# Layer zero's experts with the hidden values produced transposed: up weights loaded per tile, scaling moved to ACT

## What is computed

```python
xn = _rms_norm(x, scale)                                # x: the layer-normed input
ids = argmin(_dist2(xn, centroids), axis=-1)            # one of 8 experts per token
for e in range(8):
    h = einsum('bsd,dh->bsh', xn, up_w[e])              # 128 -> 512
    a, g = split(h, 2, axis=-1)                         # 256 and 256
    y = einsum('bsh,hd->bsd', a * silu(g), down_w[e])   # 256 -> 128
    out = where(ids == e, y, out)
out = out + skip
```

## Time and profile before

| | us |
|---|---|
| median of 3 runs | 1212.86 (1212.7 to 1213.04) |
| the profiled execution's own time | 1209.96 |
| its span, first to last instruction | 1207.7 |

### The profile page before, as it was taken

How to read it: one execution, slowest core, us unless ns; L and a number is a source line. 1 busy time by engine, 2 the same in 40 slices (tenths; PEclk the granted TensorE clock), 3 DMA queues, 4 the chain that set the end, 5 groups by cost and what they waited for, 6 DMA issues and landing times.

```text
span 1207.7 us, 28517 instructions
## 1 busy us (share of the span) xinstructions
PE 1069.6 (89%) x8602; PEld 685.4 (57%) x8602; DVE 958.7 (79%) x2148; ACT 879.5 (73%) x2187; POOL 790.2 (65%) x1147
## 2 busy tenths in 40 slices
PE   2666369989996689999999999999999999999986
PEld 1555247767774455656565556555555665565553
DVE  6779989979995578888887888788778788888861
ACT  2555338767875378888888888888788888888874
POOL 4476668668775366667666776677667766776641
PEclk9766689999997699999999999999999999999998
DMA  9511112112111322333233323332232223322310
GB/s 274 154 39 37 34 52 57 45 46 54 49 51 32 99 66 66 90 81 84 65 89 78 88 66 81 81 92 66 66 94 81 78 69 92 87 72 69 88 37 11
DMA packets 148172, 89.35 MB, mean 74 GB/s; under 512 B 73080, under 2 KB 137272, under 8 KB 147768
## 3 DMA queue, kind: packets, MB, share of 16 engines
q1 hardware_dynamic: 143928, 79.01, 25.0%
q0 software_dynamic: 4096, 8.53, 2.4%
HBM read 55.91 MB, written 31.47 MB: 72 GB/s over the span
## 4 chain that ended last, share of the span: by engine, by line
PE 52%; issue 5%; ACT 4%; DVE 4%; DMA 2%; POOL 0%; SPq 0%; another core or an unknown queue 0%; DVEq 0%; POOLq 0%
PE PS L1954 8%; PE PS L1944 6%; PE PS L1926 6%; PE PS L2019 5%; PE PS L2041 5%; PE PS L2033 4%; ACT PT L1800 4%; DVE bm L1590 3%; PE PS L2006 3%; PE PS L1996 3%; PE PS L1896 3%; PE PS L1968 3%; PE PS L2050 2%; PE PS L1984 2%; PE PS L1904 1%
## 5 line engine op out<-in xcount | busy, mean ns | idle before, releaser
L1590 DVE TENSOR_REDUCE bm<-PS 128x16 f32<-128x1024 f32 x256 | 312.2, 1219 | 34.4 <-PE PS L1926 27.4
L1800 ACT ACTIVATE PT<-PS 128x1024 f32<-128x1024 f32 x256 | 262.0, 1024 | 21.0 <-PE PS L1944 17.6
L1954 PE MATMUL PS<-PT,rows 128*32 128x256 f32 x2048 | 138.0, 387 | 2.2 <-ACT OT L1805 2.2
L1479 POOL TENSOR_TENSOR Pr<-Pr,linv 128x512 f32<-128x512 f32 x128 | 131.9, 1041 | 5.0
L1774 ACT ACTIVATE Pr<-PS,nmf 128x256 f32<-128x256 f32 x256 | 117.1, 473 | 0.4 <-DVE nmf L1610 0.4
L1610 DVE TENSOR_REDUCE nmf<-PS 128x4 f32<-128x1024 f32 x64 | 78.3, 1224 | 44.2 <-PE PS L2019 44.2
L1926 PE MATMUL PS<-KS,QS 48*128 48x256 bf16 x1024 | 101.4, 277 | 9.6 <-DVE bm L1590 6.3
L1944 PE MATMUL PS<-QS,KS 51*128 51x256 bf16 x1024 | 99.5, 273 | 11.0 <-ACT PT L1800 5.6
L469 POOL DMA_INDIRECT xs_dram<-rows,slot x64 | 65.6, 1025 | 40.0 <-DVEq L703 22.3
L1012 PE MATMUL PS<-S,wmix 128*128 128x256 f32 x192 | 69.8, 451 | 17.6 <-DVE diff L731 17.1
L1954 PEld LDWEIGHTS PS<-PT,rows 128*32 128x32 f32 x2048 | 54.5, 109 | 46.4 <-issue 19.6
(11 more groups left out here) (257 smaller groups left out, 2833.7 us busy)
## 6 DMA issues: line engine op xcount, KB each, us to landing
wsel<-in_qkv_w SPq DMA_DIRECT2D x128, 96.0 KB
parts_dram<-parts SPq DMA_DIRECT2D x32, 384.0 KB
QS<-parts_dram SPq DMA_DIRECT2D x64, 96.0 KB
KS<-parts_dram SPq DMA_DIRECT2D x64, 96.0 KB
xs_dram<-zero_t SPq DMA_DIRECT2D x1, 4752.0 KB, 26.2
xs_t<-xs_dram SPq DMA_DIRECT2D x72, 66.0 KB, 1.8
ys_dram<-ys_t SPq DMA_DIRECT2D x72, 64.0 KB, 1.6
QS<-parts_dram SPq DMA_DIRECT2D x64, 64.0 KB
```

The lines of the kernel that those rows point to most:

```text
L1479: pool.tensor_tensor(Pr[i][:, qt, :, :], Pr[i][:, qt, :, :], linv[:, i, qt, :].unsqueeze(2).broadcast_to([P, 2, SEQ]), ALU.mult).then_inc( ...
L1590: dve.tensor_reduce(bm[:, i // 2, :, 2 * (i % 2):2 * (i % 2) + 2, :].rearrange("p q r b -> p r q b"), bS.rearrange("p (r q b k) -> p r q b ...
L1800: act.activation(PT[i % 4][:, :, :], shifted_bank(t, i).rearrange("p (r k) -> p r k", r=2), ACT.Exp).then_inc(s_exp, 1)
L1954: last = pe.matmul(bC[j * VC:(j + 1) * VC, 0:SEQ], V2[q][:, kt, 4 * g + j, :], PT[(2 * g + j // 2) % 4][:, j % 2, kt * SEQ:(kt + 1) * SEQ] ...
```

## The change

Up weights become the stationary operand and the transposed xs the moving one, so that the hidden values come out transposed, as the down product wants them. Transposing hid on PE and its copy on ACT go. A tile's up weights are loaded by SP from DRAM into one of four buffers (`load_up`, stage -1; the expert's number is loaded into a register of SP). The token's factor can't be a scale per partition any more, so ACT scales xs first (`xsr`, stage 0) and PE transposes a turn later (stage 1), into two banks; the channel's scale is applied in ACT's copy of `xsT`. Up product and tanh move to stage 2, DVE's two instructions to stage 3. In a turn of ACT the scaling comes first. In a turn of SP the store comes first, then load, then `load_up`. `TAKE` is 21 instead of 20. The early load of `up` and its scaling by ACT go. The row holds rrms alone in column D.

```diff
+        NUP = 4
...
-        TAKE = 20
+        TAKE = 21
-        up = sb("up", [P, NE * 2 * HID])
+        up = [sb(f"up{i}", [P, 2 * HID]) for i in range(NUP)]
-        psU, psX, psH, psY, psO = PS[0:2], PS[2], PS[3], PS[4], PS[5]
+        psU, psX, psY, psO = PS[0:2], PS[2:4], PS[4], PS[5]
...
-            sp.dma_start(up[:, :], up_w).then_inc(s_we, 16)
             def load(t, h, q):
-                after(sp, s_fx, t - 2)
+                after(sp, s_xsr, t - 2)
...
+            def load_up(t, h, q):
+                after(sp, s_up, t - NUP + 1)
+                sp.load(expert_registers[q % TPS], tile_expert[0:1, bass.ds(t, 1)])
+                e = sp.snap(expert_registers[q % TPS], min_val=0, max_val=NE - 1)
+                apart(sp)
+                sp.dma_start(up[q % NUP][:, :], up_w[:, bass.ds(e * 2 * HID, 2 * HID)]).then_inc(s_upl[q % NUP], 16)
             for t in range(3):
                 load(t, 0, t)
+            sp.wait_ge(s_tab, 1)
+            load_up(0, 0, 0)
...
                 for turn in range(TPS):
+                    done = tile(quad, p, turn, LAST)
+                    if done:
+                        store(*done)
                     new = tile(quad, p, turn, -3)
                     if new and (not isinstance(new[0], int) or new[0] >= 3):
                         load(*new)
-                    done = tile(quad, p, turn, LAST)
-                    if done:
-                        store(*done)
+                    soon = tile(quad, p, turn, -1)
+                    if soon and (not isinstance(soon[0], int) or soon[0] >= 1):
+                        load_up(*soon)
...
         @block.vector
...
             def experts(quad, p, turn):
-                now = tile(quad, p, turn, 2)
+                now = tile(quad, p, turn, 3)
-                    after(dve, s_fh, t - 2)
+                    after(dve, s_dn, t - 2)
...
         @block.scalar
...
             def experts(quad, p, turn):
                 now = tile(quad, p, turn, 0)
                 if now:
                     t, h, q = now
+                    act.wait_ge(s_xs[q % 3], arrivals(h, q))
+                    after(act, s_fx, t - 2)
+                    act.activation(xsr[q % 3][:, 0:D], xs_t[q][:, 0:D], ACT.Identity, scale=xs_t[q][:, D:D + 1]).then_inc(s_xsr, 1)
+                now = tile(quad, p, turn, 1)
+                if now:
+                    t, h, q = now
                     act.wait_ge(s_fx, t + 1)
                     after(act, s_up, t - 2)
-                    act.copy(xsT[q % 3][:, :], psX[:, 0:P]).then_inc(s_xsT, 1)
-                now = tile(quad, p, turn, 3)
...
-                    act.copy(hidT[q % 3], psH[:, 0:2 * P]).then_inc(s_hidT, 1)
+                    act.activation(xsT[q % 3][:, :], psX[q % 2][:, 0:P], ACT.Identity, scale=scale_c[:, 0:1]).then_inc(s_xsT, 1)
...
         @block.tensor
...
             def transposes(quad, p, turn):
-                now = tile(quad, p, turn, 0)
+                now = tile(quad, p, turn, 1)
-                    pe.wait_ge(s_xs[q % 3], arrivals(h, q))
-                    after(pe, s_xsT, t)
-                    pe.transpose(psX[:, 0:P], xs_t[q][:, 0:D], ident[:, :]).then_inc(s_fx, 1)
-                now = tile(quad, p, turn, 3)
...
-                    for c in range(2):
-                        last = pe.transpose(psH[:, c * P:(c + 1) * P], hid[q % 3][:, c * P:(c + 1) * P], ident[:, :])
-                    last.then_inc(s_fh, 1)
+                    pe.wait_ge(s_xsr, t + 1)
+                    after(pe, s_xsT, t - 1)
+                    pe.transpose(psX[q % 2][:, 0:P], xsr[q % 3][:, 0:D], ident[:, :]).then_inc(s_fx, 1)
...
-                now = tile(quad, p, turn, 1)
+                now = tile(quad, p, turn, 2)
-                    e = pe.snap(experts_of[q], min_val=0, max_val=NE - 1)
+                    pe.wait_ge(s_upl[q % NUP], 16 * (G // NUP * h + q // NUP + 1))
                     pe.wait_ge(s_xsT, t + 1)
                     after(pe, s_hid, t - 1)
-                    pe.matmul(psU[q % 2][:, :], xsT[q % 3][:, :], up[:, bass.ds(e * 2 * HID, 2 * HID)],
-                              start=True, stop=True).then_inc(s_up, 1)
+                    for c in range(2 * HID // P):
+                        last = pe.matmul(psU[q % 2][:, c * P:(c + 1) * P], up[q % NUP][:, c * P:(c + 1) * P], xsT[q % 3][:, :],
+                                         start=True, stop=True)
+                    last.then_inc(s_up, 1)
```

More of the change, by code:

```diff
@@ L248, in layer_zero @@
         xsT = three("xsT", [P, P])
-        gate, hid, hidT = ([work[:, (3 * k + i) * HID:(3 * k + i + 1) * HID] for i in range(3)] for k in range(3))
+        gate, hid, xsr = ([work[:, (3 * k + i) * HID:(3 * k + i + 1) * HID] for i in range(3)] for k in range(3))
         ys_t = three("ys_t", [P, D])
@@ L289, in layer_zero @@
         s_tab = sem("tile_table_ready")
-        s_ups = sem("up_scaled")
+        s_upl = [sem(f"up_loaded{i}") for i in range(NUP)]
         s_xs = [sem(f"xs_loaded{i}") for i in range(3)]
+        s_xsr = sem("xs_scaled")
         s_fx = sem("xs_transposed")
@@ L411, in store @@
                 sp.dma_start(ys_dram[bass.ds(t * P, P), :], ys_t[q % 3][:, :]).then_inc(s_ys[q % 3], 16)
+            expert_registers = [sp.alloc_register(f"up_expert{i}") for i in range(TPS)]
+            def load_up(t, h, q):
[4 more added lines that the diff above has]
+                sp.dma_start(up[q % NUP][:, :], up_w[:, bass.ds(e * 2 * HID, 2 * HID)]).then_inc(s_upl[q % NUP], 16)
             for t in range(3):
                 load(t, 0, t)
+            sp.wait_ge(s_tab, 1)
+            load_up(0, 0, 0)
             def load_weights():
@@ L910, in experts @@
                     after(act, s_ys[q % 3], arrivals(h, q) - 16)
-                    act.activation(ys_t[q % 3][:, :], psY[:, 0:D], ACT.Identity, scale=xs_t[q][:, D + 1:D + 2]).then_inc(s_y, 1)
-                now = tile(quad, p, turn, 1)
+                    act.activation(ys_t[q % 3][:, :], psY[:, 0:D], ACT.Identity, scale=0.5).then_inc(s_y, 1)
+                now = tile(quad, p, turn, 2)
                 if now:
@@ L916, in experts @@
                     after(act, s_hid, t - 2)
-                    act.activation(gate[q % 3][:, :], psU[q % 2][:, HID:], ACT.Tanh, scale=xs_t[q][:, D:D + 1]).then_inc(s_gate, 1)
+                    act.activation(gate[q % 3][:, :], psU[q % 2][:, HID:], ACT.Tanh, scale=0.5).then_inc(s_gate, 1)
             def scalings(k):
@@ L1055, in products @@
                     e = pe.snap(experts_of[q], min_val=0, max_val=NE - 1)
-                    pe.wait_ge(s_hidT, t + 1)
+                    pe.wait_ge(s_hid, t + 1)
                     after(pe, s_y, t)
                     for c in range(2):
-                        last = pe.matmul(psY[:, 0:D], hidT[q % 3][:, c * P:(c + 1) * P], down[:, bass.ds(e * 2 * D + c * D, D)],
+                        last = pe.matmul(psY[:, 0:D], hid[q % 3][:, c * P:(c + 1) * P], down[:, bass.ds(e * 2 * D + c * D, D)],
                                          start=(c == 0), stop=(c == 1))
```

21 lines of the change are left out of this document (3 added, 18 removed).

## The result

The changed kernel took 1196.23 us (median, 1194.63 to 1201.35), the kernel before 1212.78 in the same series. The ratio is 0.9866, with a 95% interval of 0.9837 to 0.9895, so 12.7 to 19.8 us faster, 16.5 at the median. The forecast was 1198.0, in a range of 1192.5 to 1205.

What follows compares the result with a forecast made beforehand. A circuit through PE and ACT, 8.35 us a step in layer zero with DVE close behind, was taken as the bound. Hole −5.1, cadence −8.1, start −2.0, end +0.3 sum to −14.9: from 1212.86 to 1198.0 us, range 1192.5 to 1205.

Steps and rivals of the forecast that it cites:

- The hole: Between steps 20 and 21, POOL's wait for expert-output stores before its first gather goes: 5.1 us saved, bounds 4 and 5.3.
- side remark: Moving the gather to step 21 and putting stores ahead of loads on SP were each said to remove POOL's wait.
- The cadence: Layer zero's expert steps fall from 8.35 to 8.0 us: 23 steps at 0.35 save 8.1, bounds 3.5 and 11.5.
- The start: Step 11: PE opens with receptance, without waiting for xs, and ACT has less to do: 2.0 us saved, bounds 0 and 4.2.
- The circuit: A loop through PE and ACT, with hid's transposes waiting for the hidT copy, was said to set 8.35 us a step.
- Its new length: The PE and ACT loop after the change, through xsr, transpose, products, tanh and exponents: 7.91 us a step.
- DVE: DVE needs 7.69 us a step plus 4.5 for first tokens over 21 steps: 7.90 a step, close to the circuit.
- the added 0.1: Added per step because limits of 7.91 and 7.90 don't wholly absorb each other's late steps, giving 8.0 us.
- rival A: DVE or POOL take more than counted in layer zero: cadence 8.2, total −10.1 us, time 1203; chance 0.18.
- rival C: PE's weight loads in the up product are exposed: about 1269 us, or 1229 with half exposed; chance 0.03.
- The loads of up: SP's 256 KB up load per tile lands in 2.7 us, within slack of 6.1, so costs 0.
- Rival B: Better than counted, DVE needing nearer 7.4 and xsr shorter: cadence 7.85, total −19 us, time 1194; chance 0.15.

Runs made afterwards that it cites:

- e1: Kernel before with only TAKE 21 instead of 20 (first-token gather a step later): 1204.86 us, ratio 0.9967.
- e3: Changed kernel with TAKE back at 20 (gather in step 20 again): 1198.90 us, ratio 0.9913.
- e12: Changed kernel unaltered, run again on another chip: 1186.39 us, ratio 0.9890.
- e2: Kernel before with ACT's copy of the values moved behind turn 2's xsT and hidT copies: 1208.89 us, ratio 0.9995.
- e8: Kernel before with PE's register load of tile numbers moved to the top of the step: 1208.31 us, ratio 0.9977.
- e7: Changed kernel with PE's register load of tile numbers moved to the top of the step: 1195.31 us, ratio 0.9860.
- e4: Changed kernel with four experts' up weights loaded once and no up loads per tile: 1194.61 us, ratio 0.9871.
- e9: Changed kernel with PE's register load at the top of the step and TAKE 25 instead of 21: 1182.74 us, ratio 0.9854.
- e5: Changed kernel with ACT's scaling of turn 2 moved ahead of the exponent instructions: 1197.82 us, ratio 0.9884.
- e10: Changed kernel with TAKE 25 instead of 21 alone: 1185.99 us, ratio 0.9884.
- e11: Changed kernel with PE's register load at the top of the step and TAKE 26 instead of 21: 1183.67 us, ratio 0.9857.

## Why the prediction was right, and where it was not

- **The hole**: 5.1 forecast; 5.1 between the steps, 4.6 at the start of layer one (e1). Right. The side remark that either half of the edit removes it was wrong: with the store first and the gather in step 20, 4.3 of it stay (e3).
- **The cadence**: 8.0 forecast. Measured from K's projection in step 12 to that in step 32 it is (340.45 − 179.03) / 20 = 8.07, where before it was 8.39 with the hole taken out. 23 steps at 0.35 were to give 8.1 us; 20 steps gave 6.4, and the stretch from step 32 to layer one another 0.95 (31.16 for 32.11), which holds the last two of them and the end, for which I had charged 0.3. The 0.35 didn't apply everywhere: in the kernel before, DVE had no wait left from its scan at 302.72 to the one at 345.12, five steps with the first tokens' work, and took 42.40; the same five steps take 42.42 after (298.79 to 341.21). None of the 6.4 comes from these five.
- **The start**: 2.0 forecast, 1.7 measured (K of step 12 at 179.03 for 180.72).
- Together −14.2 for layer zero where −14.9 stood. The other 2.3 of the 16.5 at the median have no place in the change. That they are layer one's spread, or the chip's, is not shown; on e12's chip the same comparison gives 13.7 (11.2 to 15.2).
- **The circuit was named wrongly.** The prediction's step "psH is one bank: the turn's transposes wait for the copy" saw a real wait, but one that lay behind a longer way: ys_t, register load, up product. e2 took my wait away and nothing moved; e8 moved the register load and the step fell to 8.15. The 0.55 in the earlier trace rows between the down product (324.95) and the up product (325.50) had been taken as part of the down product, while the earlier trace rows itself has 0.44 for down in turn 1. That difference of 0.11 was the trace of the load.
- **Its new length came out, 7.90 for 7.91, partly by luck.** From PE's transpose at 206.44 to K's projection at 211.02 are 4.58 us where the sum had 4.43 (0.11, 2.51, 1.75 and 0.06), nearly all of it the gap of 0.69 for 0.55, which nothing in the sum foresaw. Against it stand 2.41 for tanh and exponents (2.50 in the sum), and 0.46 for xsr and the handover (0.52).
- **DVE** has 7.69 a step and the first tokens' work on top, as forecast, but as a limit it was put too low, and the reason for the added 0.1 was wrong. The two limits got in each other's way by 0.5 us in 20 steps, not by 0.1 in each. What filled the difference was work not counted: 2.4 us of small work in steps 13 to 17, and 5.3 for the first tokens in place of 4.5 (L765 takes 0.79 and 0.87 in the two steps with a gating, for 0.36). 153.8 + 2.4 + 5.3 is 161.5, 8.08 a step, where the forecast had 7.90 for DVE, then 8.0. That the 8.0 came near 8.07 is luck in this: 0.1 for one cause stood where another cost about twice that. It is rival A's direction (DVE more than counted), at less than A's size. e7 shows it from the other side: 0.24 off the plain steps gave 0.6 to 1.1 us in all.
- **The up product in four blocks**: 0.89 forecast for eight pairs, 0.90 measured; weight loads are 192 ns long each and hidden:

```profile
L1074 PEld LDWEIGHTS PS<-xsT,up 128*128 128x128 f32 x576 | 70.0, 192 | 6.5 <-issue 5.8 <-DMA up<-in_up_w 0.5
```

So rival C was out. A load and a multiply together take 0.11 here, as the earlier trace rows had it for the down product, though one load alone is 192 ns long.
- **The loads of up** landed in 2.9 (2.7 forecast) with one wait of 0.5 in 72, where none was forecast, and e4 prices them at nothing. **xsr**: 405 ns on average, 382 taken. **The start of PE's transpose behind xsr**: 0.06, where 0.14 was said.
- Rival B, better than counted, isn't reached even by e9 with its two further edits: 17.3 faster than the kernel before on its chip, for B's 19, and 7.91 a step from 12 to 32, for 7.85. It needed the register load moved, which none of my rivals had.

## What to carry to other kernels

When two chains of waits are nearly equally long, the one that the profile shows as a wait need not be the one that decides. Compare the same pair of instructions in a turn where nothing stands between them (0.44) and in the one in question (0.55, 0.69), and look in the program for what has no row of its own. A register load that stands behind a wait in the engine's program is such a thing: put ahead of the waits, it took 0.25 off the plain step in both kernels.

And before shortening the leading circuit, add up the next engine's work over the whole stretch, special steps included. An engine that the profile never shows waiting over 20 steps has set their length, even where the plain steps of another engine are longer: here that sum, 161.5 of 162.0, said that no more than 0.5 could be gained.

## What the runs showed of the hardware that wasn't expected

A factor given per partition lengthened ACT's instruction in all three places: tanh over 128x256 took 480 ns with the scale from an SBUF column and 385 with a constant, ys_t over 128x128 382 ns and 275, and xsT over 128x128, a plain copy before, 276 ns and 363 with the channel's scale. Tanh before, then tanh and ys_t after:

```profile
L917 ACT ACTIVATE expert_work<-PS,xs_t 128x256 f32<-128x256 f32 x72 | 34.6, 480 | 24.0 <-PE PS L1072 24.0
```

```profile
L929 ACT ACTIVATE expert_work<-PS 128x256 f32<-128x256 f32 x72 | 27.7, 385 | 29.0 <-PE PS L1074 28.9
...
L923 ACT ACTIVATE ys_t<-PS 128x128 f32<-128x128 f32 x72 | 19.8, 275 | 13.0 <-PE PS L1060 10.1 <-DMA ys_dram<-ys_t 2.7
```

So ACT got lighter although it took over the scaling: 29.2 us of xsr and 6.3 more for xsT (26.1 for 19.8), against 28.6 for the hidT copy, 6.9 from tanh and 7.7 from ys_t.

Layer one, with the same code, took 821.9 and 827.6 in the profiles of before and after, 825.5, 819.3, 817.6 and 822.1 in e1 to e4 on their chip, 823.1 to 824.7 on that of e5 to e8, and 811.0, 811.1, 811.6 and 810.6 in e12, e10, e9 and e11 on theirs. For e12 I had expected 817 to 828. So one profiled span can be 5 us off for a part that wasn't touched, and a change in one stage is better judged by that stage's own end.
